# Layer norm, attention and a ternary feed-forward layer on eight cores: x chunks that wait for V's first weights, and 24 places for the residual

## The reference

```python
B, T, D, H, d_ff = 8, 2048, 1024, 16, 4096
xn = layernorm(x)                                   # no scale, eps 1e-5
q, k, v = xn @ Wq.T, xn @ Wk.T, xn @ Wv.T           # 16 heads of 64
att = softmax((q k^T) / 8 * pmask) v                # pmask: 1 inside a block, sigmoid(w) between
h = relu(xn @ quantize(W1).T + b1)                  # quantize: to -1, 0, 1 by mean |W|
f = h @ quantize(W2).T + b2
out = x + att * silu(f)
```

## Time and profile before

| what | us |
|---|---|
| median of 3 runs | 1008.33 (1008.04 to 1009.1) |
| the profiled execution, its own time | 1008.84 |
| span of its slowest core, core 7 | 1007.1 |
| spans of all cores | 1002.1 to 1007.1 |
| PE busy in the span | 970.5 (96%) |
| DVE, ScalarE, POOL busy | 698.8, 627.3, 27.0 |

### The profile page before, as it was taken

How to read it: one execution, slowest core, us unless ns; L and a number is a source line. 1 busy time by engine, 2 the same in 40 slices (tenths; PEclk the granted TensorE clock), 3 DMA queues, 4 the chain that set the end, 5 groups by cost and what they waited for, 6 DMA issues and landing times.

```text
span 1007.1 us, 20701 instructions; the slowest of 8 cores (1002.1 to 1007.1 us)
## 1 busy us (share of the span) xinstructions
PE 970.5 (96%) x6676; PEld 350.5 (35%) x6676; DVE 698.8 (69%) x995; ACT 627.3 (62%) x739; POOL 27.0 (3%) x54
## 2 busy tenths in 40 slices
PE   2999989999999999999999999999999999999996
PEld 1443323333333333333333333333333333444442
DVE  3847889886677667767766776677667776742576
ACT  2666676667767766776677677767776775033322
POOL 0000000000000000000000000000000000000321
PEclk9999999999999999999999999999999999999999
DMA  8685687883110211120112111111101111242799
GB/s 199 173 206 185 234 275 251 217 238 67 44 43 23 48 38 43 43 43 23 43 43 44 43 40 36 32 43 43 33 22 43 43 43 43 63 122 67 188 293 252
DMA packets 30662, 99.95 MB, mean 99 GB/s; under 512 B 3680, under 2 KB 3680, under 8 KB 30304
## 3 DMA queue, kind: packets, MB, share of 16 engines
q1 hardware_dynamic: 20800, 75.56, 24.6%
q0 software_dynamic: 5152, 14.68, 7.6%
q10 hardware_dynamic: 4608, 8.39, 2.6%
HBM read 96.52 MB, written 8.39 MB: 104 GB/s over the span
## 4 chain that ended last, share of the span: by engine, by line
PE 94%; DMA 2%; issue 1%; DVE 1%; ACT 1%; DVEq 0%; ACTq 0%; POOLq 0%
PE PS L366 23%; PE PS L382 23%; PE PS L444 14%; PE PS L460 14%; PE PS L346 6%; PE PS L338 6%; PE PS L478 3%; PE PS L354 3%; PE PS L401 2%; DMA arena<-wvb 2%; ACT arena L548 1%; PE PS L379 1%; DVE arena L610 1%; DMA arena<-xP 0%; DVE arena L622 0%
## 5 line engine op out<-in xcount | busy, mean ns | idle before, releaser
L548 ACT ACTIVATE arena<-PS 128x1024 bf16<-128x1024 f32 x512 | 498.5, 1020 | 230.4 <-PE PS L444 229.6
L382 PE MATMUL PS<-arena 128*128 128x512 bf16 x1024 | 240.3, 380 | 0.0
L366 PE MATMUL PS<-arena 128*128 128x512 bf16 x1024 | 237.8, 380 | 0.0
L444 PE MATMUL PS<-arena 64*128 64x512 bf16 x1024 | 160.8, 382 | 6.6 <-ACT arena L548 5.8
L460 PE MATMUL PS<-arena 128*32 128x512 bf16 x2048 | 157.6, 384 | 0.0
L382 PEld LDWEIGHTS PS<-arena 128*128 128x128 bf16 x1024 | 93.5, 98 | 135.8 <-issue 34.1
L366 PEld LDWEIGHTS PS<-arena 128*128 128x128 bf16 x1024 | 92.3, 98 | 138.9 <-issue 40.7
L701 DVE TENSOR_TENSOR arena<-arena 128x1024 bf16<-128x1024 bf16 x200 | 136.3, 681 | 0.4 <-ACT arena L548 0.4
L655 DVE TENSOR_SCALAR arena<-PS,arena 128x512 bf16<-128x512 f32 x96 | 71.9, 749 | 67.0 <-PE PS L366 66.9
L690 DVE SCALAR_TENSOR_TENSOR arena<-arena 128x1024 bf16<-128x1024 f32 x64 | 82.2, 1284 | 34.8 <-PE PS L366 24.7
L444 PEld LDWEIGHTS PS<-arena 64*128 64x128 bf16 x1024 | 36.5, 94 | 125.8 <-issue 122.8
(11 more groups left out here) (54 smaller groups left out, 541.2 us busy)
## 6 DMA issues: line engine op xcount, KB each, us to landing
arena<-w1b SPq DMA_DIRECT2D x16, 1024.0 KB, 6.8
arena<-w2b SPq DMA_DIRECT2D x16, 1024.0 KB, 7.1
arena<-w1b SPq DMA_DIRECT2D x32, 512.0 KB, 4.6
arena<-w2b SPq DMA_DIRECT2D x32, 512.0 KB, 4.5
arena<-xP SPq DMA_DIRECT2D x16, 512.0 KB, 4.5
arena<-xT POOLq DMA_DIRECT2D x32, 256.0 KB, 8.6
outT<-arena ACTq DMA_DIRECT2D x32, 256.0 KB, 10.4
arena<-wvb POOLq DMA_DIRECT2D x2, 1024.0 KB, 15.8
```

What stands on the lines that cost most here:

```text
L366: mm = e.matmul(out, wz[n % QR][:, c * 128:(c + 1) * 128], xn[:, c * T + ts * 512:c * T + (ts + 1) * 512], start=(c == 0), stop=(c == DC - 1))
L382: mm = e.matmul(out, wz[n % QR][:, c * 128:(c + 1) * 128], h[:, c * T + ts * 512:c * T + (ts + 1) * 512], start=(c == 0 and not last), sto ...
L444: mm = e.matmul(bank(b + hh), kb[hp % 2][rows, kc * 128:(kc + 1) * 128], rhs, start=True, stop=True, tile_position=(64 * hh, 0))
L548: e.activation(out=pt[gi % PR][:], in_=PS[:, b:b + 1024], func=AF.Exp, scale=0.125, bias=-4.0).then_inc(a_exp, 1)
```

## The change

It has two parts. In SP's program, x chunks 2 and later (and what stands behind them there: the loads `ipw`, `b1r`, `b2r`) are issued only when V's first weights have landed. The residual gets 24 places instead of eight: places 0 to 7 lie in the attention's buffers behind `ot`, `cb` and `gb`, places 8 to 23 in `xn`. POOL issues the first eight loads when attention's last product is written, the next 16 after the last F1 unit, and the last eight when the result 24 before is written.

```diff
--- before.py
+++ after.py
@@ -33,6 +33,7 @@
 SR = 3
 GR = 3
 ER = 8
+RR = 24
 
 
 
@@ -164,7 +165,9 @@
     rcp = at(o + 4096, 512, BF16)
     o += 5120
 
-    xr = [at(o_xn + 2048 * i, 512, F32) for i in range(ER)]
+    o_xr = o_att + 2048 * (ER + 4)
+    xr = [at(o_xr + 2048 * i if i < 8 else o_xn + 2048 * (i - 8), 512, F32) for i in range(RR)]
+    assert o_xr + 2048 * 8 <= o
     ot = [at(o_att + 2048 * i, 512, F32) for i in range(ER)]
     cb = [at(o_att + 2048 * (ER + i), 512, F32) for i in range(3)]
     gb = [at(o_att + 2048 * (ER + 3) + 1024 * i, 512, BF16) for i in range(2)]
@@ -249,7 +252,7 @@
     d_wq, d_wk = sem("d_wq"), sem("d_wk")
     d_gam = [sem(f"d_gam{i}") for i in range(GR)]
     d_stg = [sem(f"d_stg{i}") for i in range(SR)]
-    d_xr = [sem(f"d_xr{i}") for i in range(ER)]
+    d_xr = [sem(f"d_xr{i}") for i in range(RR)]
     d_out = [sem(f"d_out{i}") for i in range(ER)]
 
     p_tr, p_v, p_u, p_s, p_pv, p_d = sem("p_tr"), sem("p_v"), sem("p_u"), sem("p_s"), sem("p_pv"), sem("p_d")
@@ -277,6 +280,8 @@
         for tc in range(KC):
             if tc >= XR:
                 e.wait_ge(v_xh, tc - XR + 1)
+            if tc == 2:
+                e.wait_ge(d_wv[0], 16)
             e.dma_start(out=xs[tc % XR][:], in_=xP[tc * 128:(tc + 1) * 128, :]).then_inc(d_x[tc % XR], 16)
             if tc == 0:
                 e.dma_start(out=ident[:], in_=idd[:]).then_inc(d_id, 16)
@@ -314,13 +319,15 @@
             e.wait_ge(p_u, U_OF[("Q", hp * TS - 1)] + 1)
             e.dma_start(out=wq[:], in_=wqd[hp * 128:(hp + 1) * 128, :]).then_inc(d_wq, 16)
 
-        e.wait_ge(p_u, U_OF[("F1", NQ - 1, FCQ - 1, TS - 1)] + 1)
+        e.wait_ge(v_s, NITP)
         for i, u in enumerate(LASTF2):
             dc, ts = u[2], u[3]
-            if i >= ER:
-                e.wait_ge(v_o, i - ER + 1)
-            e.dma_start(out=xr[i % ER][:], in_=xT[dc * 128:(dc + 1) * 128, ts * 512:(ts + 1) * 512]
-                        ).then_inc(d_xr[i % ER], 16)
+            if i == ER:
+                e.wait_ge(p_u, U_OF[("F1", NQ - 1, FCQ - 1, TS - 1)] + 1)
+            if i >= RR:
+                e.wait_ge(v_o, i - RR + 1)
+            e.dma_start(out=xr[i % RR][:], in_=xT[dc * 128:(dc + 1) * 128, ts * 512:(ts + 1) * 512]
+                        ).then_inc(d_xr[i % RR], 16)
 
 
     def tensor_program(e):
@@ -731,11 +738,11 @@
                             op=ALU.mult).then_inc(v_cb, 1)
 
         def result(n):
-            e.wait_ge(d_xr[n % ER], 16 * (n // ER + 1))
+            e.wait_ge(d_xr[n % RR], 16 * (n // RR + 1))
             if n >= ER:
                 e.wait_ge(d_out[n % ER], 16 * (n // ER))
             e.wait_ge(v_cb, n + 1)
-            e.tensor_tensor(out=ot[n % ER][:], in0=cb[n % 3][:], in1=xr[n % ER][:], op=ALU.add).then_inc(v_o, 1)
+            e.tensor_tensor(out=ot[n % ER][:], in0=cb[n % 3][:], in1=xr[n % RR][:], op=ALU.add).then_inc(v_o, 1)
 
         stats(0)
         for tc in range(KC):
```

## The result

The changed kernel takes 1014.8 us (median of three executions, 1014.4 to 1015.1) against 1009.1 before (median of seven, 1008.0 to 1011.3). The ratio of the means is 1.0051, 95% interval 1.0032 to 1.0069: 5.1 us slower (5.7 by the medians). Executions in which a whole die ran at a lower clock are left out of all numbers here. The profiled execution took 1014.36. The forecast was 1009.4, 1.1 us over the time before, range 1007.0 to 1013.0.

What follows compares the result with a forecast made beforehand. The PE, busy 96% of the span, was taken as the bound, so its start and end count. Delayed chunks and the end's gain left the slowest core +1.1 us: 1008.33 + 1.1 = 1009.4 us, range 1007.0 to 1013.0.

Steps and rivals of the forecast that it cites:

- What it gains: At the start: with chunks 2 and 3 no longer ahead in SP's queue, `wvb` moves packets soon after its issue.
- Rival (b): Start: late first packet is `wvb`'s own preparation, so no gain on weights; `wvb` at 18.1, about 1013 us; chance 25%.
- what q1 already holds goes first: At the start: loads already in SP's queue q1 move before `wvb` in POOL's q0; q1 moved 336 packets, q0 none.
- When `wvb` lands: V's first weights: issue 5.64 plus 1.3, 5.9 and 1.2 us gives landing at 14.0, bounds 13.2 and 18.1.
- What it costs: Start: chunk 2, issued at 14.1, lands at 19.0; V product starts at 22.6 against 21.20, 1.4 us later on core 7.
- The 3.6 us from chunk 2 to the V product: Start: statistics of chunk 2, normalise(1) and transposes of chunk 1 stand between chunk 2's landing and the first V product.
- What comes after: First V product to first score product: same chain, 47.2 us on core 7; change 1 is +1.1 us there.
- The 0.3 us for the transposes ahead: First V products: transposes right before them take part of the PE's slow time after a pause, giving back 0.3 us.
- the V product's place: Start of the PE: the first V product's start decides; from it on the chain is the same as now.
- Change 2: Residual's 24 places: cost nil, store backlog at the end removed; 0 to 0.5 us gain on slowest core, 0.3 taken.
- the banks: Last stage: eight PSUM banks give 15.5 us cover; harm from residual loads needs evictions 15 us late, under 2%.
- The sum: Whole kernel: slowest core at about 1008.2, +1.1 over 1007.1; median 1008.33 plus 1.1 gives 1009.4.

Runs made afterwards that it cites:

- e8: The change without the x chunks' wait; V's first weights issued at once, K's and Q's after chunk 3; ratio to the kernel before 1.0021.
- e1: The kernel before plus only the wait of x chunks from chunk 2 on V's first weights, no residual part; ratio to the kernel before 1.0052.
- e4: The whole change, with normalise(1) ahead of stats(2) on DVE; ratio to the kernel before 1.0034.
- e5: The whole change, with POOL issuing K's and Q's first weights only when chunk 3 has landed; ratio to the kernel before 1.0024.
- e6: The whole change with normalise(1) ahead of stats(2) and K's and Q's first weights after chunk 3; ratio to the kernel before 1.0017.
- e12: The whole change, first V product ahead of chunk 1's transposes on PE, chunk 0's copy to xn ahead of chunk 1's deviation; ratio to before 1.0075.
- e3: The whole change with the wait one chunk later: chunk 3, not chunk 2, waits for V's weights; ratio to the kernel before 1.0027.
- e11: e8 with chunk 0 not held up by chunk 1 on DVE and ScalarE, first V product ahead of chunk 1's transposes; ratio to before 1.0007.
- e10: The whole change with the wait from chunk 3 and K's and Q's first weights after chunk 3; ratio to the kernel before 1.0021.
- e2: The change without the x chunks' wait: the residual's 24 places and early loads alone; ratio to the kernel before 1.0004.
- e7: e5 without the wait of the x chunks, residual's 24 places kept; ratio to the kernel before 0.9997.
- e9: e8 with K's and Q's first weights right behind V's again; ratio to the kernel before 1.0018.

## Why the prediction was wrong, step by step

- **"What it gains": held.** With the two chunks gone from the queue, q0 has packets from 6.5 to 8.7 us on and not from 10.2 to 11.7, and on four cores `wvb` lands at 13.5 to 14.7, forecast 14.0. Rival (b) is out as a mechanism: 1.4 us after its issue `wvb` moves packets on four cores. (Its size, 1013, was the nearer one: the late cores' weights came at 17, past the 15 from which it was to decide.) How the sentence "what q1 already holds goes first" was put was too strong, as e8 shows.
- **"When `wvb` lands": failed, and this is the error that counts.** The sum took one time for all cores, with the 1.3 us of the load at 235.1 up to the first packets and the packet rate of core 6, an early core of its pair. Taken term by term, 14.0 came out on the early cores. On core 2 the weights land at 17.1: issue +0.3, first packet after 2.6 us and not 1.3 (+1.3), the packets in 7.5 us and not 5.9 (+1.6), the rest -0.2. That is +3.1 us with the rounding, and the late cores set the time. A hint stood in the trace: from first packet to landing `wvb` took 8.1 us on core 6, but 9.3 on core 7 and 10.3 on core 0 in the kernel before, there beside other loads; the sum has 7.1, the late cores of the change took 8.2 to 8.8.
- **Why a core is late: open.** Six runs have the same loads up to this point (the change, e1, e4, e5, e6, e12). In 23 of their 24 pairs the early core is that whose chunk 0 was there first, by 0.1 to 1.0 us, and in 20 its weights land 1.3 to 3.5 us ahead; in e4 and e6 three pairs are less than 1 us apart and one has the other order. But in all four pairs of the kernel before it is the core with the later chunk 0 that gets its weights first. A head start that is kept explains the one and not the other. Nor is it shown that the cores of a pair compete. All times here count from each core's own first instruction. As stored in the traces, that instruction stands at 12 us on one core of each pair and at 0.16 to 33 ms on the other, and the late core is the first kind in all 24 pairs (before, the first kind gets its weights first, in all four). If the two count from one origin, which no run shows, the neighbours didn't load at the same moment at all, and competition between them is out.
- **"What it costs", chunk 2's landing: undersized.** 5.0 us after `wvb` was forecast, 3.9 for the chunk and 1.0 for K's and Q's weights; it took 5.2 to 5.7 on the early cores, 5.85 on core 2 (+0.85) and 6.7 on core 0. e5 gives the price of those weights as 1.2 to 1.8 us. With them away the 3.9 us hold on the early cores, and the late ones take up to 1.1 more.
- **The 3.6 us from chunk 2 to the V product: held** (22.95 to 26.35, 3.4). Together: 3.1 + 0.85 - 0.2 = 3.75, and 22.6 + 3.75 = 26.35, core 2's start.
- **"What comes after": held, nearly.** 48.1 us from there to the scores on core 2, 47.9 on core 4; forecast 47.2 to 48.1 less 0.3. The 0.3 us for the transposes ahead don't show: the mean of the eight cores is 47.5 now and 47.6 before. What I read as the lower clock doesn't show in the granted clock, which is 1.00 in that stretch.
- **What I took to decide, the V product's place, doesn't by itself.** e3, e4, e11 and e12 bring it forward by 8 to 11 us at the latest core against the change, and the gain is 4.4 us at most and none in e12. What decides is the first chunk that was held back. In the six runs in which that is chunk 2, the first scores come 49.6 to 51.5 us after its statistics start, on all 48 cores, wherever the first V product starts (13.6 to 27.2). In e3 and e10, where it is chunk 3, they come 48.0 to 49.6 us after that one's, on all 16 cores. Without a wait (before, e2, e7) it is the first V product, 47.2 to 48.5 us ahead of them on 23 of 24 cores. So with the wait the chunk's landing sets the pace, and the loss of 5 us is that chunks 2 and later come late, most of all on the late core of each pair.
- **Change 2: the amount held, the reasoning had a gap.** Nothing was gained or lost (e2). The stores' backlog goes as forecast. The danger in the burst isn't the banks, for which I gave under 2%, but DVE's list: `result` waits for a store, and the next quantisation behind it makes the PE wait up to 2.5 us on three cores of e2. The two of them that end last, cores 4 and 7, take 941.6 and 942.0 us from the first scores to the end, core 2 takes 937.8, and the cores without the wait 935.9 to 938.5.
- **The sum.** +1.1 forecast. The slowest core's first scores were put at 70.3 (core 4, 68.41 + 1.9) and came at 74.5 on core 2; its rest took 938.2 us, as core 4's before. 74.46 + 938.2 = 1012.7.

None of the kernels tried beats the kernel before.

## What to carry to other kernels

A load that is put ahead of others is paid for by what it holds back: find the instruction, on every engine, that stands behind the first thing held back, and count from the landing of that. When a kernel runs on all cores, size a transfer by the slowest core of the kernel before, since that core sets the time; a rate from a fast core is a bound and no estimate, and so is the time up to the first packet. When several chains start side by side, look which interval is the same on every core and in every variant: it starts at what decides. An engine that is started earlier and then pauses again may pay its slow start twice.

## What the runs showed of the hardware

- The same load of 1 MB on chip (2 MB in HBM) with hardly any other load's data beside it lands 8.3 to 9.1 us after its issue on one core of a pair and 10.9 to 11.2 on the other. The first packet comes 1.4 us after the issue on the one and 2.4 to 2.7 on the other, and in the 3 us from 9 to 12 they move 0.64 to 0.65 MB and 0.47 to 0.50 (cores 2 to 5). Issued at 1.56, beside the first chunks, it lands within 0.3 us on all cores in e8, but 1.7 us apart on cores 6 and 7 in e9.
- After a pause the first eight V products take 2.8 to 3.6 us instead of 1.89, and a second pause brings it back in e4 (6.8 us of it) and e12. On core 4 of e11, where the PE paused only 0.6 and 1.7 us between its work, the second eight took 1.89. The granted clock is 1.00 in both stretches; that of e12:

```profile
26.00:33.00 7.00, 5.31 (x25) 2.87 (x26) 5.86 (x12) 2.92 (x5) 0.00 (x0) 1.00 0.66 178
```

(core 4 of e12: PE, PEld, DVE, ACT and POOL busy, granted clock, DMA share, GB/s)

- Of round-robin between queues, the rule weighed in the prediction: e8 shows both queues moving beside each other, 47 packets of q0 and 43 of q1 from 8 to 11 us on core 4. The stretch in which q0 had none is one in which q1 was filled first. Both are seen; what decides between them isn't.
- 256 KB stores that take 2.4 to 3.2 us with the queues empty take 16.5 to 20.4 (median of a core) in e2 beside the burst of loads of the same size, against 14.0 beside the slower supply of before.
